# A graph network on one core: TensorE's row fetch by five one-hots in place of a 25-block bank, and edge fields kept in SBUF

## The reference, cut to what matters

```python
def _L0_gnn_ref(inputs, edge_weight, W_self, W_neigh, b_neigh, src, dst):
    for l in range(2):
        msg = h[src] * edge_weight[:, None]
        h_neigh = segment_sum(msg, dst) * inv_deg
        h = h @ W_self[l].T + h_neigh @ W_neigh[l].T + b_neigh[l]
# L1: m = h[src] * (a_mu + exp(a_ls) * edge_attr); agg = segment_sum(m, dst)
# L2: e = leaky_relu(xl[src] + xr[dst]); softmax over a destination's edges; 5 heads of 64
# L3: alpha = leaky_relu(qn[etype, dst] + kn[etype, src]); softmax; out = xw[etype, src]
```

## Time and profile before

| | |
|---|---|
| three runs | 11,397.69, 11,404.53, 11,395.51 us; median 11,397.69 |
| profiled execution | 11,410.16 us, span 11,408.1 us |
| PE / DVE / ACT / POOL busy | 6,336 / 6,968 / 1,665 / 5,958 us |
| mean granted TensorE clock | 0.627 of full speed |
| transfers | 1,719 MB, mean 151 GB/s |

### The profile page before, as it was taken

One profiled execution on the slowest core, in us unless ns is written; L12 is line 12 of the kernel. 1 busy time (PEld: TensorE's weight loads), 2 busy tenths in 40 slices (PEclk: granted clock), 3 DMA queues, 4 the chain that ended last, 5 costly groups with the idle time before them and its releaser, 6 DMA issues. The chain is left out here.

```text
span 11408.1 us, 146167 instructions
## 1 busy us (share of the span) xinstructions
PE 6336.2 (56%) x31639; PEld 4385.4 (38%) x31640; DVE 6968.2 (61%) x9723; ACT 1664.8 (15%) x5751; POOL 5957.6 (52%) x6263
## 2 busy tenths in 40 slices
PE   1777777676666764555276455544743332923327
PEld 1555454444444432222166222224732221722226
DVE  6777545577767767777888677778941112711118
ACT  0222344200000001000065100004610000000000
POOL 2777677577767735666200266640007775057760
PEclk8666778666666656666555566665555555855558
DMA  2333444444444426888388388865923333333333
GB/s 66 93 91 92 111 124 126 102 122 120 116 110 122 121 64 209 261 263 263 96 350 333 124 263 262 264 189 216 388 103 87 85 85 67 98 91 85 85 78 105
DMA packets 983109, 1719.05 MB, mean 151 GB/s; under 512 B 527619, under 2 KB 597268, under 8 KB 929127
## 3 DMA queue, kind: packets, MB, share of 16 engines
q1 hardware_dynamic: 577360, 1118.77, 28.7%
q0 software_dynamic: 227424, 434.31, 17.6%
q10 hardware_dynamic: 178256, 165.14, 4.4%
HBM read 1271.04 MB, written 448.16 MB: 151 GB/s over the span
## 5 line engine op out<-in xcount | busy, mean ns | idle before, releaser
L537 POOL DMA_INDIRECT gathered_rows<-node_table,stage x2912 | 2800.0, 962 | 1245.8 <-issue 874.4
L537 POOL DMA_INDIRECT gathered_rows<-xl_table,stage x1664 | 1572.9, 945 | 1916.3 <-DMA stage<-slots 1436.6
L537 POOL DMA_INDIRECT gathered_rows<-rel_table,stage x1664 | 1570.1, 944 | 1908.4 <-DMA stage<-slots 1401.8
L557 PE MATMUL ps_sum<-messages,onehots 128*125 128x65 f32 (+3 forms) x13312 | 2209.2, 339 | 529.2 <-DVE messages L1654 246.3
L557 PEld LDWEIGHTS ps_sum<-messages,onehots 128*125 128x125 f32 x13312 | 2154.3, 254 | 660.8 <-issue 655.3
L680 PE MATMUL ps_G<-table_parts,low_onehots 125*128 125x400 bf16 x4992 | 1551.3, 486 | 818.7 <-DVE low_onehots L691 797.2
L1420 PE MATMUL ps_Z<-xr_parts,onehots_turned 125*128 x4992 | 1293.5, 437 | 1116.1 <-DVE z L1446 1067.3
L698 DVE TENSOR_TENSOR rows_by_feature<-ps_G,high_onehots 128x400 f32<-128x400 f32 x1664 | 944.3, 574 | 1159.0 <-PE ps_G L680 1126.4
L1532 PE MATMUL ps_Q<-query_parts,onehots_turned 125*128 x4992 | 655.3, 205 | 1486.9 <-DMA onehots_turned<-onehots_turned 1484.4
L1420 PEld LDWEIGHTS ps_Z<-xr_parts,onehots_turned 125*128 125x128 bf16 x4992 | 654.4, 131 | 1755.9 <-issue 1350.8
L680 PEld LDWEIGHTS ps_G<-table_parts,low_onehots 125*128 125x128 bf16 x4992 | 587.1, 128 | 1606.0 <-issue 1183.8
(11 more groups left out here) (297 smaller groups left out, 5087.8 us busy)
## 6 DMA issues: line engine op xcount, KB each, us to landing
stash_a<-gathered_rows SPq DMA_DIRECT2D x208, 1300.0 KB
kept_rows<-stash_a SPq DMA_DIRECT2D x208, 1300.0 KB
onehots<-onehots_kept SPq DMA_DIRECT2D x520, 500.0 KB
onehots_turned<-onehots_turned SPq DMA_DIRECT2D x416, 250.0 KB
stash_r<-gathered_rows ACTq DMA_DIRECT2D x208, 272.0 KB
kept_rows<-stash_r SPq DMA_DIRECT2D x208, 272.0 KB
onehots_kept<-onehots ACTq DMA_DIRECT2D x104, 500.0 KB
gathered_rows<-node_table,stage POOLq DMA_INDIRECT x2912
```

The lines of the kernel that those rows point to most:

```text
L537: pool.indirect_dma_start(G[:, HALF * k + q, 0:width], None, table, bass.IndirectOffsetOnAxis(stage[:, k, field, q:q + 1], 0)).then_inc(ga ...
L557: return nc.tensor.matmul(ps_sum[0:BN, bass.ds(at, width)], S[:, j, :], M, start=False, stop=True, skip_group_check=True)
```

## The change

1. `slots`, `rec` and `stage` go. The source index, weight, low part, high part and a new field, the high part divided by five (SRC_FIFTH), stay in SBUF as `src_all`, `weight_all`, `low_all`, `high_all`, `fifth_all`, edge on partition, chunk on the free axis. Several of these, with other early tensors, are released after the mask phase. Only source-with-type and type go to DRAM (`types`, 7 KB per partition, one store in the setup) and come back in a new block before the relation layers.
2. POOL reads its indices from a small tile, which ScalarE copies from `src_all` per group; POOL waits itself for free buffers (done chunks, sums, stashes) and for the copy.
3. The row of the fetch is found as block = 5b + a. The one-hot is over low part + 125a for a = 0..4 (640 elements, the comparands in PSUM), so five one-hots select the place and a, and TensorE adds up 5 x 3 matmuls in one PSUM bank of 64 x 5 = 320 columns. VectorE multiplies by a one-hot of b (5 wide) and adds up the five. The products alternate two PSUM banks between groups.
4. The row loads for the one-hots wait on SP for the one-hot four groups back instead of following the record load.

```diff
-        slots = nc.dram_tensor("slots", [NG, P, R * HALF], I32, kind="Internal").ap()
+        types_dram = nc.dram_tensor("types", [P, 2, NS], I32, kind="Internal").ap()
...
-                    sp.dma_start(slots.rearrange("g p r -> p g r"), rec[:, :, :, :].rearrange("p g a e -> p g (a e)")).then_inc(s_slotD, 16)
+                    sp.dma_start(types_dram, kept).then_inc(s_slotD, 16)
...
-                        if a == DLOC:
-                            nc.scalar.activation(dloc[:, :], ps_turn[:, a % 2, 0:NS], ACT.Copy)
-                        dest = rec[:, :, a, :] if a in (SRC, SRC_TYPE, BLOCK) else rec[:, :, a, :].bitcast(F32)
+                        dest = (src_all[:, :], kept[:, 0, :], dloc[:, :], weight_all[:, :], low_all[:, :], high_all[:, :],
+                                kept[:, 1, :].bitcast(F32), fifth_all[:, :])[a]
...
-                    link(v.tensor_copy(fin[:, BLOCK, :, :], be[:, 0, :].unsqueeze(2).to_broadcast([P, NT, C])))
+                    fifth = fin[:, SRC_FIFTH, :, :]
+                    link(v.tensor_scalar(fifth, high, float(FIVE), None, ALU.is_ge))
+                    for b in range(2, FIVE):
+                        link(v.scalar_tensor_tensor(fifth, high, float(FIVE * b), fifth, ALU.is_ge, ALU.add))
+                    link(v.scalar_tensor_tensor(over[:, :, :], fifth, -float(FIVE * BN), a_src, ALU.mult, ALU.add))
...
-        def stage_group(sp, stage, i, k, others=()):
...
+        def chunks_free(engine, i, k):
+            engine.wait_ge(chunk_done.sem, chunk_done.at((i - 1) * U + HALF * (k + 1)))
+        def rows_free(pool, i, k):
+            chunks_free(pool, i, k)
+            pool.sem_inc(pool_seen, 1)
+            pool.wait_ge(stashed[k].sem, stashed[k].at(16 * i))
+        def keep_index(act, IDX, index, i, k):
+            nc.scalar.activation(IDX[:, k, :], index[:, bass.ds(i * U + HALF * k, HALF)], ACT.Copy).then_inc(index_kept.sem, 1)
...
-                    pool.wait_ge(staged[k].sem, staged[k].at(16 * i + 16))
+                    free(pool, i, k)
+                    pool.sem_inc(pool_seen, 1)
+                    pool.wait_ge(index_kept.sem, index_kept.at(K * i + k + 1))
                     pool.sem_inc(pool_seen, 1)
...
         def load_low_row(sp, LR, i, k):
+            sp.wait_ge(low_made.sem, low_made.at(K * (i - 1) + k + 1))
...
-            for t in range(BANKS):
-                pe.wait_ge(bank_picked.sem, bank_picked.at(BANKS * n + t - 1))
-                for part in range(3):
-                    last = nc.tensor.matmul(ps_G[:, t % 2, 0:WIDE * NB], OT[0:BN, k, :],
-                                            HP[:, part, WIDE * t:WIDE * (t + 1), :].rearrange("p f b -> p (f b)"),
-                                            start=part == 0, stop=part == 2)
+            for g in range(FETCH):
+                pe.wait_ge(bank_picked.sem, bank_picked.at(FETCH * n + g - 1))
+                for a in range(FIVE):
+                    for part in range(3):
+                        last = nc.tensor.matmul(ps_G[:, (FETCH * k + g) % 2, 0:D * FIVE], OT[0:BN, k, g, a, :],
+                                                HP[:, part, a, :, :].rearrange("p f b -> p (f b)"),
+                                                start=a == 0 and part == 0, stop=a == FIVE - 1 and part == 2)
...
-            v.tensor_scalar(OT[0:BN, k, :], LR[0:BN, k, :], part[0:BN, 0:1], None, ALU.is_equal).then_inc(low_made.sem, 1)
-            dve.wait_ge(staged[k].sem, staged[k].at(16 * i + 16))
-            v.tensor_scalar(HI[:, k, :], pos[:, 0:NB], stage_f[:, k, SRC_HI, HALF - 1:HALF], None, ALU.is_equal).then_inc(high_made.sem, 1)
+            v.tensor_tensor(OT[0:BN, k, :, :, :], LR[0:BN, k, :].rearrange("p (g e) -> p g e", e=P).unsqueeze(2).to_broadcast([BN, FETCH, FIVE, P]),
+                            ids[0:BN, 0:FIVE].unsqueeze(1).unsqueeze(3).to_broadcast([BN, FETCH, FIVE, P]), ALU.is_equal).then_inc(low_made.sem, 1)
+            v.tensor_tensor(HI[:, k, :, :], pos[:, 0:FIVE].unsqueeze(1).to_broadcast([P, FETCH, FIVE]),
+                            fifth_all[:, bass.ds(i * U + HALF * k + HALF - FETCH, FETCH)].unsqueeze(2).to_broadcast([P, FETCH, FIVE]),
+                            ALU.is_equal).then_inc(high_made.sem, 1)
+            chunks_free(dve, i, k)
...
+            for g in range(FETCH):
+                v.tensor_tensor(BR[:, (FETCH * k + g) % 2, :, :], ps_G[:, (FETCH * k + g) % 2, 0:D * FIVE].rearrange("p (f b) -> p f b", b=FIVE),
+                                HI[:, k, g, :].unsqueeze(1).to_broadcast([P, D, FIVE]), ALU.mult).then_inc(bank_picked.sem, 1)
+                v.tensor_reduce(G[:, HALF * k + HALF - FETCH + g, :], BR[:, (FETCH * k + g) % 2, :, :], AX, ALU.add).then_inc(row_picked.sem, 1)
...
-                                sp.wait_ge(stashed[slot].sem, stashed[slot].at(16 * ahead))
-                                sp.sem_inc(sp_seen, 1)
-                                stage_next(ahead, slot)
+                                load_turned(sp, ST, ahead, slot)
...
+                        def added_and_stashed(pool, i, k):
+                            pool.wait_ge(z_made.sem, z_made.at(4 * (K * (i - 1) + k + 1)))
+                            pool.sem_inc(pool_seen, 1)
+                            pool.wait_ge(stashed[k].sem, stashed[k].at(16 * i))
...
+                                if m % 4 == 3:
+                                    act.wait_ge(gathered[m // 4].sem, gathered[m // 4].at(16 * HALF * (i + 1)))
+                                    keep_index(act, IDX, src_all, i + 1, m // 4)
...
+        kept_types = sb("kept_types", [P, 2, NS], I32)
+                sp.dma_start(kept_types[:, :, :], types_dram).then_inc(types_back, 16)
```

More of the change, by code:

```diff
@@ L39 @@
 PER = 7
-WIDE = 16
-BANKS = D // WIDE
+FETCH = 1
+FIVE = 5
 BANK = 512
@@ L50 @@
 FAR = -1e30
-SRC, SRC_TYPE, BLOCK, DLOC, WEIGHT, SRC_LO, SRC_HI, TYPE = range(8)
+SRC, SRC_TYPE, DLOC, WEIGHT, SRC_LO, SRC_HI, TYPE, SRC_FIFTH = range(8)
 assert NCH * C >= E + NB * C and NCH % U == 0 and NS >= NCH
@@ L489, in build @@
         coef_made = Counted("coefficients_made")
-        staged = [Counted(f"staged_{k}") for k in range(K)]
         gathered = [Counted(f"gathered_{k}") for k in range(K)]
@@ L705, in picks_over @@
                 c.over(16 * TURNS)
-            for c in (low_made, high_made, row_picked):
+            for c in (low_made, high_made):
                 c.over(GROUPS)
-            for c in (bank_made, bank_picked):
-                c.over(BANKS * GROUPS)
+            for c in (bank_made, bank_picked, row_picked):
+                c.over(FETCH * GROUPS)
             table_split.over(1)
@@ L756, in _ @@
                     def _(pool):
-                        gather_loop(pool, stage, G, D, node_table, SRC, HALF - 1)
+                        gather_loop(pool, G, D, node_table, IDX, chunks_free, HALF - FETCH)
                     @block.scalar
                     def _(act):
+                        for k in range(K):
+                            keep_index(act, IDX, src_all, 0, k)
                         with act.Fori(0, TURNS) as i:
@@ L994, in _ @@
                                          skip_group_check=True).then_inc(finished, 1)
-                for c in (*staged, *onehots_in):
+                for c in onehots_in:
                     c.over(16 * TURNS)
                 for c in gathered:
-                    c.over(16 * (HALF - 1) * TURNS)
+                    c.over(16 * (HALF - FETCH) * TURNS)
                 for c in attr_loaded:
@@ L1001, in attribute_sums @@
                 chunk_done.over(NCH)
+                index_kept.over(GROUPS)
                 for c in (msg_made, coef_scaled, coef_made):
@@ L1482, in _ @@
                         turn(TURNS - 1, True)
-                for c in (*staged, *loaded, *stashed):
+                for c in (*loaded, *stashed):
                     c.over(16 * TURNS)
@@ L1488, in pair_scores, with relation_scores @@
                     c.over(NCH // 2)
+                index_kept.over(GROUPS + K)
                 for c in (mult_made, reduced, scored):
                     c.over(NCH // QD)
-        def relation_scores(SCORE, XQ):
+        def relation_scores(SCORE, XQ, src_type, types):
             phase[0] += 1
@@ L1537, in _ @@
                     def _(act):
+                        for k in range(K):
+                            keep_index(act, IDX, src_type, 0, k)
                         with act.Fori(0, TURNS) as i:
@@ L1860, in build, with _ @@
             dense(H[:, :, :], D, [wfc[:, :]], take, None, after)
+        kept_types = sb("kept_types", [P, 2, NS], I32)
+        types_back = sem("types_back")
+        with nc.Block() as block:
+            @block.sync
+            def _(sp):
+                sp.dma_start(kept_types[:, :, :], types_dram).then_inc(types_back, 16)
+                sp.wait_ge(types_back, 16)
         norm_phase()
```

203 lines of the change are left out of this document (103 added, 100 removed).

## The result

The kernel before took 11,396.6 us (median of 4 runs), the changed one **11,111.2 us** (4 runs, 11,108.8 to 11,114.2): a ratio of 0.9749, 95% interval 0.9732 to 0.9766, 285 us less. The forecast was 11,072, 39 us too low, and its range held the time. The profiled execution after has a span of 11,111.2 us against 11,408.1, 296.9 less.

A forecast was written before the change was run, and what follows sets the result against it. The prediction took POOL's gathers as the bound; -50 - 16 - 238 - 18 - 10 + 6.5 = -325.5 us took the profiled 11,410.2 to 11,084.7. Less 12.5 for the runs' median, it forecast 11,072 us, range 11,018 to 11,195.

The forecast's parts named there:

- The bound: All eight gather loops: POOL's gathers set the time, with a floor of 1.248 us each, boundaries included.
- the pair scores: Both pair loops: waits for record loads queued behind the stash go away, -120 and -118 us.
- The allowance of 5 us a loop for DMA: Pair loops: taken as 1,045 us each against the floor of 1,038, with DMA named as what could be late next.
- The attribute sums: Both attribute sum loops: the shorter fetch chain falls under POOL's 8.73 us a group, 935 to 910, -25 us twice.
- Weighted sum 1: First weighted sum loop: gathers stretched beside the one-hot of L691 become normal, -16 us, ends 0 and -40.
- Starts, setup, types: Outside the loops: earlier first gathers -18 us, cheaper setup -10, loading the types back +6.5.
- the half of the pair loops: Pair loops' poorer end: only half of the gain of -127 and -125 us if the queues fill.
- A: Rival, pair loops: transfers bind and half of 238 us is lost, whole 11,191 us; chance 0.12.
- B: Rival, weighted sums: TensorE stays at the low clock and paces them, +35 and +13, whole 11,120 us; chance 0.10.
- C: Rival, group boundaries: POOL's added instructions are no longer covered, up to +250 us, whole 11,322; chance 0.06.
- D: Rival, fetch in attribute and weighted sums: TensorE's weight loads become exposed, +722 us, whole 11,860; chance 0.04.
- E: Rival, pair loops: no gain, because POOL then waits as long for the stash, whole 11,310 us; chance 0.03.

The follow-up runs named there:

- e11: e10 with weighted sum 1's large one-hots reading positions from PSUM (912.5 us) and an unused 32 KB load behind each stash in pair loop 2 (1,164.3 us).
- e12: Kernel before, TensorE left out of weighted sum 1 and pair loops, record load ahead of the stash in pair loop 1 only: 1,085.4 us; pair loop 2 1,162.5.
- e10: Changed kernel with TensorE left out of weighted sum 1 and the pair loops: weighted sum 1 986.9 us, pair loops 1,039.8 each, whole 11,112 us.
- e2: Kernel before, weighted sum 1's three large one-hots reading one comparand from PSUM, on a slow chip: 13,683 us against 13,658 unedited.
- e6: Repeat of e2, the kernel before with the PSUM comparand in weighted sum 1, on a slow chip: 13,669 us.
- e5: Changed kernel, weighted sum 1's three large one-hots reading one comparand from PSUM, on a slow chip: 13,359 us against 13,346 unedited.
- e9: Changed kernel, unedited, on a slow chip: 13,346 us against 13,658 for the kernel before, ratio 0.9777.

## Why the prediction was right, and where it missed

**The bound and the pair scores: right.** POOL's floor holds, 1.248 us a gather in the relation loops as before, and the pair loops went to it with no boundary wait at all, -126 and -125 for -120 and -118. e11 shows the mechanism by itself: put one small load behind the stash and 125.6 us come back. What was too simple is "behind it on the same queue": by e12 the order on the queue is 77 us, and 47 come with the load being issued at that time at all. It also lands later than the prediction's "some 11 us after POOL finished group n": 12.9 us after that group's last gather was issued. The allowance of 5 us a loop for DMA was not needed: 0.89 of share and 289 GB/s (291 forecast) delayed nothing. POOL's waits in pair scores 1 of the changed kernel (one long wait ahead of the loop, and the usual gaps):

```profile
POOL gathered_rows L553 <- issue: 253.2, 831, 0.3
POOL gathered_rows L553 <- PEq L1440: 214.9, 1, 214.9
```

**The attribute sums: right in what they came to**, -23 and -22 for -25. 15 matmuls took 4.18 us at the low clock level (granted clock 0.50 in this stretch), as forecast, and a group that had not to wait for gathers would take 8.3 us, under 8.73.

```profile
2400.46 3.60 PEld L704 LDWEIGHTS ps_G<-table_parts,low_onehots 125*128 125x128 bf16 x15 [2.89 <-issue]
2400.46 4.18 PE L704 MATMUL ps_G<-table_parts,low_onehots 125*128 125x320 bf16 x15 [2.76 <-DVE low_onehots L715]
```

One-hots at 2399.52 and again at 2408.39 are 8.87 apart, 0.57 of it a wait for gathered rows. The loads run beside the matmuls. POOL's late starts at boundaries were 27 us in attribute sum 1 before and are none after. That the shorter chain did it, and not the fields that POOL no longer waits for, is argued from these rows and not shown on a fast chip.

**Weighted sum 1: the step that failed.** "Where one runs beside the one-hot of L691 it takes 1.07 instead of 0.94 us ... sums to 16 us" and "another 24 us are 59 gathers beside the three large one-hots, which stay". The 1.07 were held by the block-row one-hot that ended just after the gather began. And the 24 did not stay: how much is held depends on where in the one-hot a gather starts. The term was -16 and came out +26, 42 us of the error. The step that failed is the premise that the held time goes by which small instruction runs beside a gather, and that the rest stays when VectorE's work shrinks; it goes by which large operation the gather starts in, and where. The ends (0, -40) had no loss in them, although the prediction had a rule that could have given one: the Trainium skill (SBUF — State Buffer, Who interferes with whom) says that a VectorE instruction with two SBUF inputs contends with a GpSimd instruction that reads SBUF. The prediction applied it to the new five-wide one-hot alone. In this case's traces it holds for the large ones that were there all along, 0.61 us a gather in e10 and 0.00 in e11. The statement of the same section of the Trainium skill that tensor_scalar can lock the shared ports, which the prediction laid under its 16 us, shows here for L691 too, but only in gathers that start 0.08 to 0.13 us into it and by at most 0.07 us (e2, e6). The five-wide one-hot, for which the prediction allowed some loss, held none of 20 gathers that started in it.

**Starts, setup, types.** The first gather came 13.6 us earlier (-13.3 forecast). The other gaps gave -13.3 for -8.2: -9.8 and -9.9 behind the two attribute sums, which had no term: in the first of them the last chunk sums started 17 us after POOL's last gather before and 9 after. +4.6 behind pair scores 1 had no term either, and its cause is open; +4.0 behind pair scores 2 is where the types come back (+6.5 with a start of -2 forecast; the load took 4.5 us, and no row shows the 1.5 to enter a block). The other gaps gave -2 to +2.

**The sum.** -296.9 in the profiled executions against -325.5: +42 from weighted sum 1, -13 from the pairs, -5 from the gaps, +5 from the attribute sums. The forecast was 39 us too low and not 29, because the profiled execution stood 12.5 us above the median before and 1.8 after. That the time still fell between the ends of the forecast's terms is in part luck: +42 met -18 from terms that gave more than forecast. And these ends, 11,018 to 11,115, are narrower than the terms say: added up plainly they reach from about 11,010 to 11,170, without the half of the pair loops.

**The rivals.** A: no, pair loops at the floor. B: no, weighted sum 2 stayed at 911 with a clock of 0.78. C: no, relation loops at 1.248. D: no, the loads above. E: no, POOL shows no wait in the pair loops but its issue gaps (the rows above). The loss came from a rival that wasn't named.

**A version that should be faster than both** is the changed kernel with the comparand in PSUM (e5). On a slow chip it was no faster than the changed kernel. On a fast one only e11 against e10 was run, with TensorE left out: 74 us in that loop. With TensorE in place I estimate the loop at weighted sum 2's 912 in place of 974, 62 us; that was not measured.

## What to carry to other kernels

When the bound engine's instructions vary in length, list for each long one what ran when it *started*, and test the candidates by their ends: here one formula met 197 gathers to a hundredth of a microsecond, while the neighbour that ran beside the gather in the row had no part in it. Work taken off an engine that isn't the bound moves what is left of it in time, so give such a term both signs. And a small load that an engine waits for should not stand on a queue behind a large transfer, nor be issued only when a step's own rows have landed: keep the field resident, or load it steps ahead.

## What the runs showed of the hardware

- A GpSimd indirect gather of 0.94 us that starts inside a VectorE tensor_tensor with two SBUF inputs is longer by what is left of that operation less 0.12 us. One that starts ahead of the operation, or in its first 0.02 us, is not held (6 such gathers in the changed kernel took 0.94 us). With one of the two inputs in PSUM nothing is held (206 gathers in e11), and the operation takes the same 1.20 us.
- A tensor_scalar of 125 x 128 (0.28 us, one tensor and a value per partition from SBUF) holds by the same formula, but only gathers that start 0.08 to 0.13 us into it, for at most 0.07 us (7 gathers of weighted sum 1 in e2 and e6).
- A load of 32 KB issued 0.7 us after a stash of 1,300 KB on the same queue let its waiter start only at 6725.40, 6 us after it was issued and 1.67 us past its turn, in a loop that moves about 261 GB/s; over 104 groups that made 125.6 us. Behind such a stash 32 KB land 5.2 us after their issue, ahead of it 2.3 us (e12).
- Chips ran the same program in 11,397 and in 13,658 us. On a slow one TensorE stood 805 times, 883 us in all, ahead of its matmuls in one loop of 104 groups (e9); the cause is open.
